# Picked layers of a four-layer residual kernel: loops over single steps, half-wide row hand-offs and single row and product buffers

## The chip, the cores and the metric

The kernel runs on one core of a Trainium2 chip. The metric is the device time of one execution in microseconds. Times of single instructions, waits and chains come from one profiled execution of the kernel.

## The reference, cut to what matters

`x` is 32 sequences of 64 rows of 1024 values. Four residual layers follow each other: `x + conv(x)` (a long convolution with a generated kernel), `x + x·W1[id1]ᵀ`, `x + x·W2[id2]ᵀ`, and a gated MLP with rank-16 adapters. The change touches the second and third, the "picked" layers:

```python
def _L1_cond_ref(x, adapter_ids, weight):
    w = weight[adapter_ids]                      # (32, 1024, 1024), one of 16 matrices per sequence
    return jnp.einsum('bsi,boi->bso', x, w)
...
x = x + _L1_cond_ref(x, itok_B_0_15, L1_cond_weight)
x = x + _L2_cond_ref(x, L2_cond_weight, itok_B_1_14)
```

Each sequence picks one of 16 matrices of 1024 x 1024. With the inputs that `setup_inputs(0)` draws, the picks are

```text
itok_B_0_15 12 10 13 8 7 5 2 8 12 3 7 3 15 8 2 1 12 12 7 10 13 9 8 14 7 11 10 14 8 0 8 10
            sequences per matrix 0..15: 1 1 2 2 0 1 0 4 6 1 4 1 4 2 2 1
itok_B_1_14 9 7 13 9 6 11 2 4 7 6 5 4 8 3 3 9 14 11 12 11 10 9 10 4 14 11 13 4 5 6 9 3
            sequences per matrix 0..15: 0 0 1 3 4 2 3 2 1 5 2 4 1 2 2 0
```

## The kernel before, in words

**Steps.** During the convolution VectorE builds a table on the chip: sequences with the same pick are put together in pairs, and each pair (or a left-over single one, with a spare sequence beside it) is a step. A step loads one matrix (4 MB, in four chunks of 1 MB) and multiplies the 2 x 64 = 128 rows of its pair with it. A table line per layer holds the matrix and the two places in `X` for every step; lines beyond the last real step point at spare rows and at matrix 0. `count_turns` (L1244 on) finds the number of **turns**, of two steps each, as the highest step number halved and rounded up. All engines loop over turns, with `half` 0 and 1 in a turn.

**Arithmetic.** Each fp32 factor is cut into a high part (ScalarE: `wh`, `rh`, one copy to the type for fast matmuls) and the rest (VectorE: `wl`, `rl`, a subtraction); TensorE adds up three products, high·high, high·low and low·high. A chunk is 4 blocks of 128 x 512, so 12 matmuls of 512 columns; a step is 48.

**A step on each engine, before.**
- SP (L387 to L402) waits for VectorE's cut of the same chunk of the step before (`w_lo`) and loads the chunk into `W[:, c]`.
- ScalarE (`picked_turn`, L758): cut chunk 0 (L741), cut the rows of the step (L755, two activations of 128 x 512), copy the first half of the last step's product out of PSUM (L746), cut chunk 1, copy the second half, cut chunks 2 and 3.
- VectorE: cut chunk 0 (L1302), the rows (L1315, two), chunks 1 and 2, add the last step's result to `X` (L1325, two), chunk 3.
- TensorE (`picked_turn`, L1766): chunk 0, eight transposes of the last step's product (L1762), chunks 1, 2, 3.

The host lays the matrix out so that chunks 0 and 1 make the first half of the output and chunks 2 and 3 the second; each output half has a PSUM bank, and `rh`, `rl`, `prod` and these banks exist twice, for `half` 0 and 1. The rows are therefore needed whole from chunk 0 on, and the rows' second half is read up to chunk 3. The order of the work is the order written in each engine's program; the engines meet through counting semaphores. `step_added` holds ScalarE back from the rows of the next layer until the last step of this one is in `X`.

**After the picked layers** `rows_done` (L1332) releases two 4 MB stores of `X` on SP, and ScalarE and VectorE begin to cut the MLP's operands. POOL sets the identity matrix for the transposes when the convolution ends.

Of the kernel before, what the change touches and what calls it, by code (L numbers as in the profile page):

```python
# [48 lines left out]
assert STEPS % 2 == 0 and STEPS <= B  # L49
# [74 lines left out]
def build(nc, ins, out):  # L124
    with ExitStack() as ctx:
# [24 lines left out]
        turns = sb(early, "turns", [2, 1], I32)  # L150
# [43 lines left out]
        with ExitStack() as s:  # L194
            ident = sb(s, "ident", [P, P])
            wh = sb(s, "wh", [P, WC, WK, WN], F32R)
            wl = sb(s, "wl", [P, WC, WK, WN], F32R)
            rh = sb(s, "rh", [P, 2, LT, 2 * H], F32R)
            rl = sb(s, "rl", [P, 2, LT, 2 * H], F32R)
            prod = sb(s, "prod", [2 * H, 2, L])  # L200
            sb(s, "gap", [P, (region + REGION - nc.sbuf_base) // 4])
            W = sb(s, "W", [P, WC, WK, WN])
# [86 lines left out]
        turned = sem("turned")  # L289
        step_added = sem("step_added")  # L290
# [55 lines left out]
        def _(sp):  # L346
# [44 lines left out]
            for layer, w in enumerate((ins["w1"], ins["w2"])):  # L391
                count = sp.value_load(turns[layer:layer + 1, 0:1], min_val=B // 4, max_val=STEPS // 2)
                with sp.Fori(0, count) as it:
                    for half in range(2):
                        pick = sp.value_load(table[layer:layer + 1, 0, bass.ds(it * 2 + half, 1)],
                                             min_val=0, max_val=NPICK - 1)
                        for c in range(WC):

                            sp.wait_ge(w_lo, (it * 2 + (before + half)) * WC + (c + 1))
                            sp.dma_start(W[:, c], w[bass.ds(pick, 1), c].rearrange("a p i o -> (a p) i o")  # L400
                                         ).then_inc(w_in[c], 16)
                before = before + count * 2  # L402
# [303 lines left out]
        def _(act):  # L706
# [36 lines left out]
            def copy_product(g, half, o):  # L743

                act.wait_ge(chunk_done, g * WC + (2 * o + 2 + WC))
                nc.scalar.activation(prod[:, half, o * WN:(o + 1) * WN], bank(2 * half + o),  # L746
                                     ACT.Copy).then_inc(prod_copied, 1)

            def step_rows_hi(s, half, added):

                seqs = [act.value_load(table[layer:layer + 1, 1 + k, bass.ds(s, 1)],
                                       min_val=0, max_val=B + SPARE - 1) for k in range(2)]
                act.wait_ge(step_added, added)
                for k, seq in enumerate(seqs):
                    nc.scalar.activation(rh[:, half, :, k * H:(k + 1) * H],  # L755
                                         X[:, bass.ds(seq, 1)].rearrange("p a l h -> p (a l) h"),
                                         ACT.Copy).then_inc(rows_hi, 1)

            def picked_turn(it, base, first):

                for half in range(2):
                    s = it * 2 + half
                    g = base + s
                    lag = not (first and half == 0)
                    if lag:
                        cut_chunk(g, 0)
                        step_rows_hi(s, half, g + 1)
                        copy_product(g - 1, 1 - half, 0)
                    cut_chunk(g, 1)
                    if lag:  # L770
                        copy_product(g - 1, 1 - half, 1)
                    cut_chunk(g, 2)
                    cut_chunk(g, 3)
# [3 lines left out]
            for layer in range(2):  # L777
                count = act.value_load(turns[layer:layer + 1, 0:1], min_val=B // 4, max_val=STEPS // 2)
                step_rows_hi(0, 0, base + 2)
                if layer == 0:  # L780
                    cut_chunk(0, 0)
                picked_turn(0, base, True)
                with act.Fori(1, count) as it:
                    picked_turn(it, base, False)
                base = base + count * 2
                copy_product(base - 1, 1, 0)
                if layer == 0:
                    cut_chunk(base, 0)
                copy_product(base - 1, 1, 1)
# [268 lines left out]
        def _(dve):  # L1058
# [185 lines left out]
            def count_turns():  # L1244
# [41 lines left out]
            stages = [number_steps, count_turns, find_members, place_members]  # L1286
# [8 lines left out]
            V.memset(tick[:, 2:3], 0.0).then_inc(chunk_done, WC)  # L1295
            V.memset(tick[:, 3:4], 0.0).then_inc(step_added, 2)
# [8 lines left out]
            def place(s, k):  # L1305
                return dve.value_load(table[layer:layer + 1, 1 + k, bass.ds(s, 1)],
                                      min_val=0, max_val=B + SPARE - 1)

            def step_rows_lo(s, g, half):

                for k in range(2):
                    seq = place(s, k)
                    dve.wait_ge(rows_hi, g * 2 + (k + 1))
                    mine = slice(k * H, (k + 1) * H)
                    V.tensor_tensor(out=rl[:, half, :, mine],  # L1315
                                    in0=X[:, bass.ds(seq, 1)].rearrange("p a l h -> p (a l) h"),
                                    in1=rh[:, half, :, mine].bitcast(F32), op=ALU.subtract).then_inc(rows_cut, 1)

            def add_step(s, g):

                for k in range(2):
                    seq = place(s, k)
                    dve.wait_ge(turned, g + 1)
                    rows = X[:, bass.ds(seq, 1)].rearrange("p a l h -> p (a l) h")
                    ins_ = V.tensor_tensor(out=rows, in0=ps[:, TURN:TURN + 2].rearrange(  # L1325
                        "p c (l w) -> p (c l) w", w=2 * H)[:, :, k * H:(k + 1) * H], in1=rows, op=ALU.add)
                ins_.then_inc(step_added, 1)

            dve.wait_ge(table_ready, 1)
            base = 0  # L1330
            for layer in range(2):
                count = dve.value_load(turns[layer:layer + 1, 0:1], min_val=B // 4, max_val=STEPS // 2)  # L1332
                step_rows_lo(0, base, 0)
                if layer == 0:
                    cut_chunk(0, 0)
                for half in range(2):
                    if half == 1:
                        cut_chunk(base + 1, 0)
                        step_rows_lo(1, base + 1, 1)
                    cut_chunk(base + half, 1)  # L1340
                    cut_chunk(base + half, 2)
                    if half == 1:
                        add_step(0, base)
                    cut_chunk(base + half, 3)
# [705 lines left out]
```

## Time and profile before

| | us |
|---|---|
| median of 3 runs (2216.17 to 2218.48) | 2217.92 |
| the profiled execution, its own time | 2217.24 |
| its span | 2215.6 |
| TensorE busy, share of the span | 96% |
| VectorE busy, share of the span | 73% |

TensorE's clock is given as a share of full speed. TensorE's mean granted clock over the run was 0.99. "Idle before, releaser" in a row is the time that the engine had nothing to run before the instruction, and what ended it; the chain of waits follows the work back from the last instruction, each piece with the time by which it moved the end. Matmuls overlap each other, so in the timeline each seems to last longer than the distance to the next one; the chain shows the distance.

### The profile page before, as it was taken

The page shows a single profiled execution, that of the slowest core. Times are in us where ns is not written, and L with a number is a line of the kernel's source. Part 1 is how long each engine was busy: PE and PEld are TensorE (multiplying, and loading weights), DVE is VectorE, ACT ScalarE, POOL GpSimd, SP SyncE. Part 2 cuts the span into 40 slices and gives each one's busy share as a digit, 9 for nine tenths or more (in the row PEclk, how much of TensorE's full clock was granted, in tenths as well). Part 3 has the DMA queues.
Part 4 walks back from the last instruction along what each step waited for, and adds up shares of the span by engine and source line. Part 5 has one row for each costly group of instructions (what it writes and reads, how often), then busy time and mean ns, then how long its engine had stood idle before and what let it go on. Part 6 is the DMA issues. An engine that isn't in the chain of part 4 may idle for free.

```text
span 2215.6 us, 33884 instructions
## 1 busy us (share of the span) xinstructions
PE 2118.8 (96%) x10544; PEld 1793.9 (81%) x10544; DVE 1625.9 (73%) x2079; ACT 975.7 (44%) x1222; POOL 98.9 (4%) x167
## 2 busy tenths in 40 slices
PE   2998999999998799999999999999999999999998
PEld 2997888878886688888888778888888888878887
DVE  7778999989997887878787336548888878753433
ACT  2222877777784533434333324334343433333332
POOL 3111000000000231000000000000000000000000
PEclk9999999999998999999999999999999999999999
DMA  5999999989997575434343895534434343365543
GB/s 192 380 363 351 349 352 352 355 306 351 352 354 302 159 203 146 108 94 113 93 111 101 250 261 189 185 121 110 107 95 107 95 106 101 84 199 171 181 152 123
DMA packets 255813, 449.90 MB, mean 203 GB/s; under 512 B 147031, under 2 KB 147223, under 8 KB 234519
## 3 DMA queue, kind: packets, MB, share of 16 engines
q1 hardware_dynamic: 242198, 417.08, 57.4%
q0 software_dynamic: 11392, 32.01, 4.4%
q10 hardware_dynamic: 2176, 0.26, 0.1%
q8 instruction: 21, 0.34, 0.1%
q14 instruction: 26, 0.20, 0.0%
HBM read 409.13 MB, written 63.73 MB: 213 GB/s over the span
## 4 chain that ended last, share of the span: by engine, by line
PE 83%; DVE 7%; SPq 3%; DMA 2%; issue 2%; ACT 2%; DVEq 0%; POOL 0%; ACTq 0%; POOLq 0%
PE ps L1791 18%; PE ps L1792 18%; PE ps L1793 18%; PE ps L1752 7%; PE ps L1754 7%; PE ps L1753 7%; PE ps L1729 3%; SPq L529 2%; PE ps L1836 2%; PE ps L1835 2%; PE ps L1762 2%; PE ps L1867 1%; PE ps L1868 1%; DMA araw<-picked_a 1%; DMA wraw<-picked_bd 1%
## 5 line engine op out<-in xcount | busy, mean ns | idle before, releaser
L1791 PE MATMUL ps<-bh,oph 128*128 128x512 f32 x1216 | 476.4, 392 | 9.5 <-ACT tmp L793 6.0
L1792 PE MATMUL ps<-bl,oph 128*128 128x512 f32 x1216 | 475.9, 391 | 0.0
L1793 PE MATMUL ps<-bh,opl 128*128 128x512 f32 x1216 | 474.3, 390 | 0.0
L1302 DVE TENSOR_TENSOR wl<-W,wh 128x2048 fp32r<-128x2048 f32 x160 | 362.3, 2286 | 28.7 <-ACT wh L741 28.7
L1366 DVE TENSOR_TENSOR tmp<-ps,tmp 128x512 f32<-128x512 f32 (+1 forms) x340 | 234.3, 690 | 132.2 <-PE ps L1836 67.2
L1363 DVE TENSOR_TENSOR wdl<-wraw,wdh 128x1024 fp32r<-128x1024 f32 x92 | 112.7, 1225 | 268.6 <-ACT wdh L793 268.6
L741 ACT ACTIVATE wh<-W 128x2048 fp32r<-128x2048 f32 x160 | 299.0, 1908 | 7.2 <-DMA W<-in_w 5.6
L1791 PE MATMUL ps<-acb_h,wdh 128*128 128x512 f32 (+1 forms) x736 | 281.3, 382 | 7.5 <-DVE acb_l L1363 7.0
L1792 PE MATMUL ps<-acb_l,wdh 128*128 128x512 f32 (+1 forms) x736 | 279.8, 380 | 0.0
L1793 PE MATMUL ps<-acb_h,wdl 128*128 128x512 f32 (+1 forms) x736 | 279.6, 380 | 0.0
L1791 PEld LDWEIGHTS ps<-bh,oph 128*128 128x128 f32 x1216 | 229.5, 189 | 55.0 <-DVE opl L1363 10.7
L1793 PEld LDWEIGHTS ps<-bh,opl 128*128 128x128 f32 x1216 | 229.0, 188 | 48.7
L1752 PE MATMUL ps<-wh,rh 128*128 128x512 f32 x640 | 257.1, 402 | 11.8 <-DVE wl L1302 7.6
L1792 PEld LDWEIGHTS ps<-bl,oph 128*128 128x128 f32 x1216 | 229.6, 189 | 42.9
L1754 PE MATMUL ps<-wh,rl 128*128 128x512 f32 x640 | 251.1, 392 | 0.0
L1753 PE MATMUL ps<-wl,rh 128*128 128x512 f32 x640 | 250.7, 392 | 0.0
L793 ACT ACTIVATE wdh<-wraw 128x1024 fp32r<-128x1024 f32 x92 | 97.4, 1059 | 313.9 <-PE ps L1793 250.1
L793 ACT ACTIVATE oph<-sraw 128x512 fp32r<-128x512 f32 x168 | 106.1, 632 | 279.8 <-PE ps L1793 152.6
L1791 PEld LDWEIGHTS ps<-acb_h,wdh 128*128 128x128 f32 x736 | 138.4, 188 | 38.7 <-DVE acb_l L1363 6.5
L1793 PEld LDWEIGHTS ps<-acb_h,wdl 128*128 128x128 f32 x736 | 138.4, 188 | 26.6
L1792 PEld LDWEIGHTS ps<-acb_l,wdh 128*128 128x128 f32 x736 | 138.4, 188 | 25.7
L1752 PEld LDWEIGHTS ps<-wh,rh 128*128 128x128 f32 x640 | 121.1, 189 | 43.3 <-issue 19.9
(204 smaller groups left out, 2843.7 us busy)
## 6 DMA issues: line engine op xcount, KB each, us to landing
W<-in_w SPq DMA_DIRECT2D x160, 1024.0 KB, 4.9
raw<-in_wgu SPq DMA_DIRECT2D x168, 256.0 KB, 2.8
wraw<-in_wd SPq DMA_DIRECT2D x84, 512.0 KB
toep<-kpad SPq DMA_DIRECT2D x32, 1024.0 KB, 8.9
lraw<-picked_b SPq DMA_DIRECT2D x88, 256.0 KB, 4.1
raw<-kept_acts SPq DMA_DIRECT2D x88, 256.0 KB, 3.5
kept_acts<-tmp SPq DMA_DIRECT2D x84, 256.0 KB, 2.3
picked_b<-in_lora_b POOLq DMA_DIRECT2D x32, 352.0 KB, 4.7
```

The costliest lines, as they stand in the source:

```text
L741: nc.scalar.activation(wh[:, c], W[:, c], ACT.Copy).then_inc(w_hi, 1)
L793: return nc.scalar.activation(to, src, ACT.Copy)
L1302: V.tensor_tensor(out=wl[:, c], in0=W[:, c], in1=wh[:, c].bitcast(F32), op=ALU.subtract).then_inc(w_lo, 1)
L1363: return V.tensor_tensor(out=to, in0=a, in1=b, op=ALU.subtract)
L1366: return V.tensor_tensor(out=to, in0=a, in1=b, op=ALU.add)
L1729: last = mm(ps[:, i % RING, (e + 1) * LT * B - n:(e + 1) * LT * B], lhsT=toep[:, i % RING, e, d * P:(d + 1) * P], rhs=rows[:, 0:n], start= ...
L1752: mm(to, lhsT=rh[:, half, at], rhs=wh[:, c, k], start=first, stop=False)
L1753: mm(to, lhsT=rh[:, half, at], rhs=wl[:, c, k], start=False, stop=False)
L1754: last = mm(to, lhsT=rl[:, half, at], rhs=wh[:, c, k], start=False, stop=end)
L1791: mm(to, lhsT=wh, rhs=mh, start=start, stop=False)
L1792: mm(to, lhsT=wh, rhs=ml, start=False, stop=False)
L1793: return mm(to, lhsT=wl, rhs=mh, start=False, stop=stop)
```

## The change

- The loops of all engines run over single steps; `count_turns` becomes `count_steps`, the highest step number plus one. The assertion that the number of table lines is even goes.
- `rh`, `rl` and `prod` exist once; the product's two PSUM banks exist once. The identity matrix moves behind them in memory.
- The host lays the chunks out anew: chunks 0 and 1 hold the first half of the input dimension (for the two output halves), chunks 2 and 3 the second. So chunks 0 and 1 read the first half of the rows alone, 2 and 3 the second half, and output half `o` is complete after chunk `2 + o`.
- ScalarE and VectorE cut a step's rows in two halves (128 x 256 each, for two sequences: four instructions instead of two), each half once the chunks that read its old content are done.
- TensorE waits for the copy of product half `o` before it writes bank `o` again, and for both copies before the transposes.
- The last step of a layer is written out: four transposes stand inside chunk 3, ahead of its last block, VectorE adds this half to `X`, and ScalarE and VectorE cut the next layer's first row half while the second half of the product is still on its way. In the last step of the first layer they also cut the next layer's chunks 0 and 1 ahead.

```diff
+            rh = sb(s, "rh", [P, LT, 2 * H], F32R)      # rl alike
+            prod = sb(s, "prod", [2 * H, L])
 SP
-                with sp.Fori(0, count) as it:
-                    for half in range(2):
-                        pick = sp.value_load(table[layer:layer + 1, 0, bass.ds(it * 2 + half, 1)],
+                with sp.Fori(0, count) as it:
+                    pick = sp.value_load(table[layer:layer + 1, 0, bass.ds(it, 1)],
 ScalarE
+            def copy_product(g, o):
+                act.wait_ge(chunk_done, g * WC + (o + 3 + WC))
+                act.wait_ge(turned, g + 1)
+                nc.scalar.activation(prod[:, o * WN:(o + 1) * WN], bank(o), ACT.Copy).then_inc(prod_copied, 1)
+            def step_rows_hi(seqs, g, half):
+                act.wait_ge(chunk_done, g * WC + (2 * half + 2))
+                mine = slice(half * WK, (half + 1) * WK)
+                for k, seq in enumerate(seqs):
+                    nc.scalar.activation(rh[:, mine, k * H:(k + 1) * H],
+                                         X[:, bass.ds(seq, 1), mine].rearrange("p a l h -> p (a l) h"),
+                                         ACT.Copy).then_inc(rows_hi, 1)
+            def picked_step(it, g):
+                cut_chunk(g, 0)
+                seqs = places(it)
+                act.wait_ge(step_added, g + 1)
+                step_rows_hi(seqs, g, 0)
+                cut_chunk(g, 1)
+                copy_product(g - 1, 0)
+                cut_chunk(g, 2)
+                copy_product(g - 1, 1)
+                step_rows_hi(seqs, g, 1)
+                cut_chunk(g, 3)
...
+                else:                                   # the second layer's first step
+                    cut_chunk(base, 0)
+                    cut_chunk(base, 1)
+                    copy_product(base - 1, 0)
+                    act.wait_ge(half_added, 1)
+                    step_rows_hi(seqs, base, 0)
+                    copy_product(base - 1, 1)
+                    cut_chunk(base, 2)
+                    act.wait_ge(step_added, base + 2)
+                step_rows_hi(seqs, base, 1)
...
+                with act.Fori(1, count) as it:
+                    picked_step(it, base + it)
+            copy_product(base - 1, 0)                   # after both layers
+            copy_product(base - 1, 1)
 VectorE
-                link(V.tensor_scalar(found[:, 0, 0:1], found[:, 0, 0:1], 0.5, 0.75, ALU.mult, ALU.add))
-                round_turns(found[:, 0, 0:1])
-                link(V.tensor_copy(turns[:], found[:, 0, 0:1]))
+                link(V.tensor_scalar_add(found[:, 0, 0:1], found[:, 0, 0:1], 1.0))
+                link(V.tensor_copy(counts[:], found[:, 0, 0:1]))
...
+            V.memset(tick[:, 7:8], 0.0).then_inc(turned, 1)
+            V.memset(tick[:, 5:6], 0.0).then_inc(rows_cut, 2)
+            V.memset(tick[:, 4:5], 0.0).then_inc(prod_copied, 3)
...
+            def picked_step(it, g):
+                cut_chunk(g, 0)
+                both = places(it, layer)
+                step_rows_lo(both, g, 0)
+                cut_chunk(g, 1)
+                cut_chunk(g, 2)
+                step_rows_lo(both, g, 1)
+                add_step(it - 1, g - 1)
+                cut_chunk(g, 3)
...
+                last = places(count - 1, layer)
+                base = base + count
                 if layer == 0:
                     cut_chunk(base, 0)
+                    cut_chunk(base, 1)
+                add_last_half(last, 0, base - 1)
+                if layer == 0:
+                    both = places(0, 1)
+                    step_rows_lo(both, base, 0)
+                    add_last_half(last, 1, base - 1)
+                    cut_chunk(base, 2)
+                    step_rows_lo(both, base, 1)
+                    cut_chunk(base, 3)
+                else:
+                    add_last_half(last, 1, base - 1)
 TensorE
+            def picked_step(g, first=False, last=False):
+                pe.wait_ge(rows_cut, g * 4 + 4)
                 pe.wait_ge(prod_copied, g * 2 + 2)
+                chunk(g, 0)
+                if not first:
+                    turn_product(g - 1)                 # waits: prod_copied (both copies), step_added
+                pe.wait_ge(prod_copied, g * 2 + 3)
+                chunk(g, 1)
+                pe.wait_ge(rows_cut, g * 4 + 6)
+                chunk(g, 2)
+                if not last:
+                    chunk(g, 3)
+                    return
+                chunk(g, 3, range(WK - 1))
+                pe.wait_ge(prod_copied, g * 2 + 4)
                 pe.wait_ge(step_added, g + 2)
+                turn_half(0).then_inc(half_turned, 1)
+                chunk(g, 3, range(WK - 1, WK))
+                pe.wait_ge(prod_copied, g * 2 + 5)
+                turn_half(1).then_inc(turned, 1)
...
+                picked_step(base, first=True)
+                with pe.Fori(1, count - 1) as it:
+                    picked_step(base + it)
+                base = base + count
+                picked_step(base - 1, last=True)
 host
-    picked = lambda w: w.reshape(NPICK, 2, WN, 2, WK, P).transpose(0, 1, 3, 5, 4, 2).reshape(
+    picked = lambda w: w.reshape(NPICK, 2, WN, 2, WK, P).transpose(0, 3, 1, 5, 4, 2).reshape(
```

## Rows read from the trace of the kernel before

**Rows 1.** The page: busy time of each engine, share of the span, instructions.

```profile
PE 2118.8 (96%) x10544; PEld 1793.9 (81%) x10544; DVE 1625.9 (73%) x2079; ACT 975.7 (44%) x1222; POOL 98.9 (4%) x167
```

**Rows 2.** Groups by line (busy us, mean ns | idle before): picked layers.

```profile
L1302 DVE TENSOR_TENSOR wl<-W,wh 128x2048 fp32r<-128x2048 f32 x160 | 362.3, 2286 | 28.7 <-ACT wh L741 28.7
L741 ACT ACTIVATE wh<-W 128x2048 fp32r<-128x2048 f32 x160 | 299.0, 1908 | 7.2 <-DMA W<-in_w 5.6 <-PE ps L1754 1.0
...
L1315 DVE TENSOR_TENSOR rl<-X,rh 128x512 fp32r<-128x512 f32 x80 | 51.7, 685 | 2.8 <-ACT rh L755 2.5
L1325 DVE TENSOR_TENSOR X<-ps,X 128x512 f32 x80 | 51.5, 683 | 8.8 <-PE ps L1762 8.5 <-issue 0.3
L746 ACT ACTIVATE prod<-ps 128x512 f32<-128x512 f32 x80 | 47.2, 590 | 100.6 <-PE ps L1754 100.6
...
L1762 PE MATMUL ps<-ident,prod 128*128 128x128 f32 x320 | 41.5, 273 | 1.5 <-ACT prod L746 1.5
```

**Rows 3.** The page, DMA issues: count, size, median us to landing.

```profile
W<-in_w SPq DMA_DIRECT2D x160, 1024.0 KB, 4.9
```

**Rows 4.** Windows: us, busy us of each engine (instructions), PE clock, DMA share, GB/s.

```profile
210.00:225.00 15.00, 15.00 (x67) 12.37 (x67) 11.93 (x8) 10.39 (x9) 0.00 (x0) 0.93 0.98 375
...
300.00:443.00 143.00, 143.00 (x675) 117.33 (x674) 135.88 (x97) 111.52 (x95) 0.00 (x0) 1.00 0.95 353
443.00:455.00 12.00, 6.97 (x32) 5.37 (x31) 6.57 (x7) 5.92 (x6) 0.00 (x0) 0.84 0.60 228
```

**Rows 5.** Chain of waits, whole run (start us, us): the transposes of single steps.

```profile
224.16 0.88 PE ps L1762 x8
236.15 0.87 PE ps L1762 x8
247.93 0.87 PE ps L1762 x8
...
438.33 0.88 PE ps L1762 x8
```

**Rows 6.** Chain of waits, 303.5 to 309.5 us: around a step's first matmul.

```profile
304.37 0.23 PE ps L1754
304.59 0.34 PE ps L1752
```

**Rows 7.** Waits from 260 to 440 us: total us, times, longest us.

```profile
ACT prod L746 <- PE ps L1754: 34.3, 15, 2.5
DVE wl L1302 <- ACT wh L741: 9.4, 16, 0.7
```

**Rows 8.** Timeline of ScalarE, 440 to 475 us: the layers' border.

```profile
451.09 1.15 ACT L755 ACTIVATE rh<-X 128x512 fp32r x2 [3.05 <-DVE X L1325]
```

**Rows 9.** Timeline of VectorE, 440 to 475 us.

```profile
450.27 0.69 DVE L1325 TENSOR_TENSOR X<-ps,X 128x512 f32 x1 [0.16 <-issue]
```

**Rows 10.** Timeline of TensorE, 440 to 460 us.

```profile
447.02 0.39 PE L1754 MATMUL ps<-wh,rl 128*128 128x512 f32 x1
448.18 1.09 PE L1762 MATMUL ps<-ident,prod 128*128 128x128 f32 x8 [0.77 <-ACT prod L746]
453.53 0.79 PE L1752 MATMUL ps<-wh,rh 128*128 128x512 f32 x1 [4.26 <-DVE rl L1315]
```

**Rows 11.** Chain of waits, 440 to 475 us: TensorE after the border.

```profile
454.32 0.43 PE ps L1753
...
457.73 0.38 PE ps L1752
```

**Rows 12.** Timelines of ScalarE, then VectorE, 680 to 706 us: the end.

```profile
692.72 0.60 ACT L746 ACTIVATE prod<-ps 128x512 f32<-128x512 f32 x1 [4.84 <-PE ps L1754]
...
695.54 0.69 DVE L1325 TENSOR_TENSOR X<-ps,X 128x512 f32 x1 [0.17 <-issue]
```

**Rows 13.** Timeline of TensorE, 743 to 765 us: a gap in the next layer.

```profile
759.96 0.47 PE L1791 MATMUL ps<-bh,oph 128*128 128x512 f32 x1 [3.48 <-ACT tmp L793]
760.26 0.40 PE L1792 MATMUL ps<-bl,oph 128*128 128x512 f32 x1
```

More of the change, by code:

```diff
@@ L48 @@
 SPARE = 3
-assert STEPS % 2 == 0 and STEPS <= B
+assert STEPS <= B
 FF = 2752
@@ L1319, in add_step, with step_rows_lo @@
-            def add_step(s, g):
[L1321 to L1326, printed above, removed]
-                ins_.then_inc(step_added, 1)
+            def step_rows_lo(both, g, half):
+                lts = slice(half * WK, (half + 1) * WK)
+                for k, seq in enumerate(both):
+                    dve.wait_ge(rows_hi, g * 4 + (2 * half + k + 1))
+                    mine = slice(k * H, (k + 1) * H)
+                    V.tensor_tensor(out=rl[:, lts, mine],
+                                    in0=X[:, bass.ds(seq, 1), lts].rearrange("p a l h -> p (a l) h"),
+                                    in1=rh[:, lts, mine].bitcast(F32), op=ALU.subtract).then_inc(rows_cut, 1)
@@ new lines, in turned_rows @@
+            def turned_rows(seq, k, at, n):
+                rows = X[:, bass.ds(seq, 1), at * WK:(at + n) * WK].rearrange("p a l h -> p (a l) h")
+                return V.tensor_tensor(out=rows, in0=ps[:, TURN + at:TURN + at + n].rearrange(
+                    "p c (l w) -> p (c l) w", w=2 * H)[:, :, k * H:(k + 1) * H], in1=rows, op=ALU.add)
+            def add_step(s, g):
+                for k, seq in enumerate(places(s, layer)):
+                    dve.wait_ge(turned, g + 2)
+                    ins_ = turned_rows(seq, k, 0, 2)
+                ins_.then_inc(step_added, 1)
@@ new lines, in add_last_half, with places @@
+            def add_last_half(both, at, g):
+                if at == 0:
+                    dve.wait_ge(half_turned, layer + 1)
+                else:
+                    dve.wait_ge(turned, g + 2)
+                for k, seq in enumerate(both):
+                    ins_ = turned_rows(seq, k, at, 1)
+                ins_.then_inc(half_added if at == 0 else step_added, 1)
+            def places(s, at):
+                return [dve.value_load(table[at:at + 1, 1 + k, bass.ds(s, 1)],
+                                       min_val=0, max_val=B + SPARE - 1) for k in range(2)]
@@ L1742, in _ @@
                     convolve(c, i)
-            def chunk(g, half, c):
-                pe.wait_ge(w_lo, g * WC + (c + 1 + WC))
-                to = bank(2 * half + c // 2)
-                for k in range(WK):
-                    at = (c % 2) * WK + k
-                    first, end = at == 0, at == LT - 1
-                    mm(to, lhsT=rh[:, half, at], rhs=wh[:, c, k], start=first, stop=False)
-                    mm(to, lhsT=rh[:, half, at], rhs=wl[:, c, k], start=False, stop=False)
-                    last = mm(to, lhsT=rl[:, half, at], rhs=wh[:, c, k], start=False, stop=end)
-                last.then_inc(chunk_done, 1)
@@ L1780, in _ @@
             for layer in range(2):
[L1781 to L1786 removed]
+                count = pe.value_load(counts[layer:layer + 1, 0:1], min_val=B // 2, max_val=STEPS)
+                picked_step(base, first=True)
+                with pe.Fori(1, count - 1) as it:
+                    picked_step(base + it)
+                base = base + count
+                picked_step(base - 1, last=True)
             def three(to, wh, wl, mh, ml, start, stop):
```

156 lines of the change are left out of this document (56 added, 100 removed).

## The prediction

> **What bounds the kernel now.** I began with the page: TensorE is busy for 96% of the span, VectorE for 73% [rows 1]. A mean hides stages, so I took the groups by line next. A step of a picked layer asks VectorE for four chunk cuts of 2286 ns, two row cuts of 685 and two adds of 683: 11.88 us if nothing overlaps; and ScalarE for 4 x 1908 and 2 x 590 ns and two row copies [rows 2]. The 160 loads of W are 40 steps, landing 4.9 us after issue [rows 3], though the picks drawn need only 19 pairs in each layer (each matrix's count halved and rounded up: 19 and 19). So one step in each layer is padding. By the windows TensorE is busy without a break from 300 to 443 us, VectorE for 135.88 of 143 us, and DMA moves 353 GB/s; a window near by reached 375 GB/s, so the loads too have only some 6% in hand [rows 4]. The chain of waits shows which limit holds: from the transposes at 224.16 to those at 438.33 us lie 18 steps, 11.90 us each [rows 5], and the pieces between are matmuls of 0.23 us, with 0.34 at the start of a loop turn [rows 6]. Steady steps are bound by TensorE. VectorE still has about 0.6 us of waiting in each (9.4 us in 15 steps), ScalarE 2.3 [rows 7]. At the border of the layers TensorE stands: ScalarE waits for VectorE's last add before it may cut rows [rows 8], which ends at 450.96 us [rows 9]; TensorE's last matmul starts at 447.02 and the next layer's first at 453.53, 6.51 us later, with eight transposes inside [rows 10]. The granted clock of that window is 0.84 [rows 4], and ten matmuls run at about 0.43 instead of 0.23 us, from 453.53 to 458.11 [rows 10, 11]: the lower level, 1.2 GHz.
>
> **The change, part by part.**
>
> *Steps.* Two of 40 steps go, TensorE's and their loads with them: 2 x 11.90 = **-23.8 us**. The padding did full work: all steps have the same length [rows 5].
>
> *Loop turns.* Every step now begins a turn, every second one did. An interval with a turn's start was 11.99 us, one without 11.78 [rows 5]; over the 18 the mean lies about 0.07 below the long ones, and the first matmul of a turn costs 0.34 - 0.23 = 0.11 us [rows 6]. TensorE also gets one more wait before chunk 0, one before chunk 1 and one before chunk 2, all on things long done; the trace has no such wait alone, so its price lies between 0 and the 0.11 of a turn's start. I take 0.1 a step for all, near the turn row: 36 x 0.1 = **+3.5 us** (0 to +8).
>
> *VectorE in a step.* Rows in halves are two instructions more. On the line through 685 ns for 512 columns and 2286 for 2048 a half takes 419 ns, fixed part 152 [rows 2]. The row sums to 11.88, yet a step of 11.90 holds 0.6 of waiting [rows 2, 5, 7], so neighbours overlap by about 0.6 over eight instructions, 0.08 each; the two extra cost 2 x (0.15 - 0.08) = 0.15 us, and busy time becomes 11.4 of 11.9. Cost nothing while 0.5 us is left. Counting from a step's start on TensorE, with matmul chunks of 2.7 and transposes of 0.9 us [rows 5, 6]: transposes end at 3.7, VectorE adds until 5.1, cuts chunk 3 until 7.3, the next step's chunk 0 until 9.5, row half 0 until 10.2, chunk 1 until 12.4, chunk 2 until 14.6 and row half 1 until 15.3, which is 3.4 in the next step, before its transposes. TensorE wants chunk 0 at 11.9, row half 1 and chunk 2 at 18.3, chunk 3 at 21.0. The cover is TensorE's own work, 2 us or more everywhere.
>
> *ScalarE in a step.* A half row copy is about 0.37 us on the line through 590 and 1908 ns [rows 2]; four are 1.5 us, and the 2.3 us of waiting hold what is added. The copy of product half 0 moves behind chunk 2 (9.3 to 9.9 us after the step's start), ahead of the bank's new use at 11.9; then chunk 2's cut until 11.8, just 0.6 before VectorE takes it. Product half 1 is complete at 12.1 and copied at 12.7; the transposes want it at 14.6. Behind it stand the second row half and chunk 3's cut, done by 15.3; VectorE takes it at 17.0. So the single buffers and banks cost 0. If ScalarE were 0.6 us later, VectorE would begin to wait.
>
> *Loads.* As many bytes a step, one queue, the same wait for VectorE's cut. By the times above chunk loads are issued at 9.5, 12.4, 14.6 and 19.2 us (before, the add stood between the last two in the same way). At 375 GB/s a chunk takes 2.8 us [rows 4], four 11.2 of 11.9; with 4.9 to landing chunk 0 lands just before ScalarE asks for it and VectorE 2 us behind that. Cost 0, at most 0.2 a step. SP's one register load a step stays.
>
> *The border.* Now half the product is turned inside chunk 3, and ScalarE and VectorE have cut the next chunks 0 and 1. From the end of the first four transposes: two half adds with their start 1.05 us, two half row copies 0.95, copy of product half 1 0.55 (it stands behind them on ScalarE), hand-over 0.15, four slow transposes 0.55 (half of 1.09 [rows 10]) and TensorE's load of the new count, some 0.25. That is 3.5 us; the four transposes and the last block put its beginning at about the old last matmul's start. Against 6.51: **-3.0 us** (-1.5 to -4). VectorE's row half is done before product half 1 is turned; late next is that copy.
>
> *The clock at the border.* TensorE's pause falls from 0.77 and 4.26 us around the transposes [rows 10] to one of about 2. The low stretch cost 4.58 us for ten matmuls, at 0.23 each 2.3 [rows 11]: **-2.2 us** if it goes, 0 if not. I take that it goes, by the nearest row below.
>
> *The end.* Before, 3.51 us from the start of the last copies (692.72) to the last add's end (696.23) [rows 12]. After: 0.44 for transposes put into chunk 3, 0.60 copy, 0.12, 0.55 transposes, 0.14, two half adds of 0.42 with the 0.17 between them [rows 12], 2.85 in all: **-0.7 us** (0 to -1.3). The MLP hangs on this add; its loads wait behind the stores of `X` released by it, so it moves as a whole.
>
> *The beginning.* Three memsets more and one register load more ahead of the first row cut, half as much row work before the first matmul: 0 (-0.5 to +0.5). The table gets shorter by some small operations, hidden by the convolution's last tiles. The moved identity is written by POOL at the same place in its queue; nothing waits for it before the second step.
>
> **Sum:** -23.8 + 3.5 - 3.0 - 2.2 - 0.7 = -26.2 us. The profiled execution took 2217.24, so 2191.0; it lies 0.7 under the median of 2217.92, so I predict **2191.7 us** for the median.
>
> **On the clock.** After a pause of 3.48 us at 759.96 the matmuls of the next layer keep 0.40 us each, as those at 447.02 do [rows 10, 13]; after 0.77 plus 4.26 with small transposes between they fall to the low level. A pause of 2 us is on the safe side of both.
>
> **Rivals.**
> 1. *The clock still falls at the border.* For: the transposes around the pause are already slow. Against: rows 13. 2191.7 + 2.2 = 2193.9.
> 2. *VectorE becomes the bound.* If nothing of its work overlapped, a step would be 4 x 2.286 + 4 x 0.419 + 2 x 0.683 = 12.18 us, 0.28 more, 38 x 0.28 = 10.7: 2202. Against: overlap is what rows 2 and 7 show together.
> 3. *Slower: the single row and product buffers put hand-overs in line.* Place: ScalarE's row copies behind the last step's product. Price: at the border, where that order is forced, add end to first matmul is 453.53 - 450.96 = 2.57 us [rows 9, 10]; in each of 38 steps it is 98 us: 2289. It decides from 26.2 / 38 = 0.7 us a step. Against: the cover of 2 us worked out above. The Trainium skill (Trainium Kernel Development and Optimization, Best Practices) asks for double buffers to overlap DMA with compute, which speaks against the change; W keeps its four chunks a step ahead, and no row shows a second row buffer in use for more than this cover.
> 4. *A turn's start gets dear.* If smaller loops fetched code at each turn, and a fetch took what the loads here take, 4.9 us [rows 3], 36 of them would be 176 us: about 2368. Against: 0.11 us at 18 such starts [rows 6]. The Trainium skill (Runtime: NRT & Kernel Launch, Instruction fetch mechanics) says that a taken branch to code outside the sequencer's window stalls for a fetch; the trace shows no such stall before.
> 5. *No step is saved* (other picks than drawn by seed 0, or a count of 20). Then 40 steps and the rest: -3.0 - 2.2 - 0.7 + 3.7 = -2.2: 2215.7, within 0.2%, which is about what a measurement of this kernel can tell from no change.
>
> **Chances.** Forecast 0.74, rival 1 0.08, rival 2 0.10, rival 3 0.02, rival 4 0.02, rival 5 0.04. Faster by over 0.2% 0.92, within 0.04, slower 0.04. Range: the low end takes turn starts at 0 and the border at its best (2187), the high end the dearer waits or rival 2 (2203).
>
> **What would show it.** 152 loads of W and 1824 matmuls of 512 columns in the picked layers; steps of 11.9 to 12.0 us between transposes; VectorE's waits now before the adds (for the transposes), some 0.5 us a step; about 3.5 us between the first layer's last matmul and the second's first, at full clock; the rest of the kernel shifted by 26 us. Steps of 12.2 with VectorE never waiting would be rival 2; TensorE waiting for row cuts or the product copy in each step, rival 3. 160 loads would overthrow the main term.

## The result, and the profile after

The changed kernel takes 2185.36 us (median of 4 runs, 2185.11 to 2187.31) against 2217.05 us for the kernel before in the same comparison (4 runs, 2214.07 to 2218.48): a ratio of 0.9853, 95% interval 0.9842 to 0.9865, so 31.7 us less, where 26.2 were forecast. The profiled execution took 2185.16 us.

The page of the changed kernel (span, busy time of the engines, the loads of W), which answers to [rows 1, 3]:

```profile
span 2183.5 us, 34214 instructions
...
PE 2087.3 (96%) x10432; PEld 1774.5 (81%) x10432; DVE 1610.3 (74%) x2144; ACT 971.2 (44%) x1282; POOL 99.0 (5%) x167
...
W<-in_w SPq DMA_DIRECT2D x152, 1024.0 KB, 6.9
```

152 loads are 38 steps: the main term is there. But a load now lands 6.9 us after its issue, not 4.9. The groups by line, answering to [rows 2], say who notices:

```profile
L1318 DVE TENSOR_TENSOR wl<-W,wh 128x2048 fp32r<-128x2048 f32 x152 | 343.6, 2285 | 9.9 <-ACT wh L742 9.0
...
L742 ACT ACTIVATE wh<-W 128x2048 fp32r<-128x2048 f32 x152 | 290.7, 1915 | 61.0 <-DMA W<-in_w 55.1 <-PE ps L1795 3.6
...
L1327 DVE TENSOR_TENSOR rl<-X,rh 128x256 fp32r<-128x256 f32 x152 | 57.3, 418 | 3.1 <-issue 2.3 <-ACT rh L759 0.7
...
L748 ACT ACTIVATE prod<-ps 128x512 f32<-128x512 f32 x76 | 44.4, 584 | 10.7 <-PE ps L1795 9.3
```

Read the right-hand side. ScalarE's wait for TensorE before the product copies fell from 100.6 us to 9.3, VectorE's for ScalarE's chunk cuts from 28.7 to 9.0, and ScalarE's wait for loads rose from 5.6 to 55.1. The half row cuts take 418 ns, as worked out. The chain of waits gives the pace, answering to [rows 5]:

```profile
225.62 0.87 PE ps L1802 x8
237.41 0.87 PE ps L1802 x8
249.19 0.87 PE ps L1802 x8
...
303.26 7.93 DMA W<-in_w
```

A step is 11.79 us (from one set of transposes to the next, and the same as mean of the 17 up to 425.89 us), not 11.9 to 12.0 as forecast, and not 11.90 as before. From 303 us on the chain runs through loads of W: they have become as late as they may be.

The border of the layers, in the timelines of TensorE, ScalarE and VectorE of the changed kernel (answering to [rows 8 to 10]):

```profile
434.35 0.65 PE L1802 MATMUL ps<-ident,prod 128*128 128x128 f32 x4
434.76 0.47 PE L1793 MATMUL ps<-wh,rh 128*128 128x512 f32 x1
438.12 0.66 PE L1802 MATMUL ps<-ident,prod 128*128 128x128 f32 x4 [2.43 <-ACT prod L748]
439.17 0.49 PE L1793 MATMUL ps<-wh,rh 128*128 128x512 f32 x1 [0.39 <-issue]
...
440.00 0.63 PE L1793 MATMUL ps<-wh,rh 128*128 128x512 f32 x1
```
```profile
431.82 1.92 ACT L742 ACTIVATE wh<-W 128x2048 fp32r<-128x2048 f32 x1 [0.72 <-DMA W<-in_w]
433.65 0.58 ACT L748 ACTIVATE prod<-ps 128x512 f32<-128x512 f32 x1
436.86 0.72 ACT L759 ACTIVATE rh<-X 128x256 fp32r x2 [2.64 <-DVE X L1334]
437.49 0.58 ACT L748 ACTIVATE prod<-ps 128x512 f32<-128x512 f32 x1
```
```profile
433.77 2.29 DVE L1318 TENSOR_TENSOR wl<-W,wh 128x2048 fp32r<-128x2048 f32 x1 [0.34 <-ACT wh L742]
435.98 0.75 DVE L1334 TENSOR_TENSOR X<-ps,X 128x256 f32 x2
```

From the last matmul of layer one (435.30) to the first of layer two it is 3.87 us against 6.51; forecast, 3.5. The half add could have begun at 435.0, when the four transposes were done. It began at 435.98, behind the cut of the next layer's chunk 1, which was late because its load was. The pause is short, and still TensorE falls to its lower clock level (matmuls 0.43 us apart instead of 0.23) 0.8 us after it has started again.

### The profile page after: what moved, and what is told of

Read it like the earlier page. It is cut to its first block, busy times and chain, and to the rows that moved or that the text cites. A ratio compares the mean times of both kernels' runs of the same rounds, so it can differ in the third digit from the quotient of the medians.

```text
span 2183.5 us, 34214 instructions
## 1 busy us (share of the span) xinstructions
PE 2087.3 (96%) x10432; PEld 1774.5 (81%) x10432; DVE 1610.3 (74%) x2144; ACT 971.2 (44%) x1282; POOL 99.0 (5%) x167
## 4 chain that ended last, share of the span: by engine, by line
PE 82%; DVE 8%; DMA 4%; ACT 2%; issue 2%; DVEq 1%; POOL 0%; ACTq 0%; SPq 0%; POOLq 0%
PE ps L1849 19%; PE ps L1850 19%; PE ps L1851 19%; PE ps L1793 4%; PE ps L1795 4%; PE ps L1794 4%; PE ps L1769 4%; DMA W<-in_w 3%; PE ps L1894 2%; PE ps L1893 2%; DVE wl L1318 2%; PE ps L1802 1%; PE ps L1925 1%; PE ps L1926 1%; DMA araw<-picked_a 1%
## 5 line engine op out<-in xcount | busy, mean ns | idle before, releaser
L1318 DVE TENSOR_TENSOR wl<-W,wh 128x2048 fp32r<-128x2048 f32 x152 | 343.6, 2285 | 9.9 <-ACT wh L742 9.0
L742 ACT ACTIVATE wh<-W 128x2048 fp32r<-128x2048 f32 x152 | 290.7, 1915 | 61.0 <-DMA W<-in_w 55.1
L1793 PE MATMUL ps<-wh,rh 128*128 128x512 f32 x608 | 242.4, 399 | 7.9 <-DVE wl L1318 7.5
L1795 PE MATMUL ps<-wh,rl 128*128 128x512 f32 x608 | 238.8, 393 | 0.0
L1794 PE MATMUL ps<-wl,rh 128*128 128x512 f32 x608 | 238.3, 392 | 0.0
L807 ACT ACTIVATE oph<-sraw 128x512 fp32r<-128x512 f32 x168 | 106.1, 632 | 282.5 <-PE ps L1851 154.2
L1769 PE MATMUL ps<-urev,toep 128*128 128x256 f32 (+7 forms) x1024 | 150.5, 309 | 1.7 <-issue 1.2
```

The costliest lines, as they stand in the source:

```text
L742: nc.scalar.activation(wh[:, c], W[:, c], ACT.Copy).then_inc(w_hi, 1)
L807: return nc.scalar.activation(to, src, ACT.Copy)
L1318: V.tensor_tensor(out=wl[:, c], in0=W[:, c], in1=wh[:, c].bitcast(F32), op=ALU.subtract).then_inc(w_lo, 1)
L1769: last = mm(ps[:, i % RING, (e + 1) * LT * B - n:(e + 1) * LT * B], lhsT=toep[:, i % RING, e, d * P:(d + 1) * P], rhs=rows[:, 0:n], start= ...
L1793: mm(bank(o), lhsT=rh[:, at], rhs=wh[:, c, k], start=first, stop=False)
L1794: mm(bank(o), lhsT=rh[:, at], rhs=wl[:, c, k], start=False, stop=False)
```

## The experiments

"Picked layers" below is the time from their first matmul to the release of the MLP (the memset of `tick` in VectorE's timeline), "border" the distance between the layers' matmuls, "slow" the matmuls more than 0.35 us apart among the first 60 after it, "MLP" from the release to the span's end. All come from the one profiled execution of each run, the medians from all its executions. e1 to e8 ran on one chip, e9 to e11 on another; for the first pair (before, changed) the chip is not on record.

| kernel | us a step | picked layers | border | slow | MLP | median, and that of before beside it |
|---|---|---|---|---|---|---|
| before | 11.90 | 487.6 | 6.51 | 10 | 1519.3 | 2217.05 |
| e1 before again | 11.90 | 487.3 | 6.50 | 9 | 1517.1 | 2219.54, 2220.31 |
| e2 chunk 2's cut ahead | 11.80 | 484.9 | 6.51 | 8 | 1517.4 | 2216.35, 2220.31 |
| changed | 11.79 | 457.9 | 3.87 | 8 | 1516.4 | 2185.36, 2217.05 |
| e3 20 steps | 11.80 | 481.3 | 3.38 | 8 | 1521.2 | 2212.20, 2220.31 |
| e4 plain border | 11.79 | 460.8 | 5.75 | 14 | 1520.5 | 2191.42, 2220.31 |
| e5 changed again | 11.79 | 457.7 | 3.78 | 7 | 1516.8 | 2185.86, 2218.86 |
| e6 copy first | 12.04 | 466.6 | 3.80 | 9 | 1519.3 | 2198.90, 2218.86 |
| e7 border reordered | 11.82 | 456.8 | 2.83 | 8 | 1520.1 | 2188.31, 2218.86 |
| e8 three loads | 11.79 | 455.7 | 2.94 | 7 | 1520.7 | 2186.25, 2218.86 |
| e9 changed, third | 11.79 | 455.8 | 3.56 | 0 | 1522.0 | 2190.64, 2219.81 |
| e10 late release | 11.79 | 455.6 | 2.94 | 0 | 1518.2 | 2187.98, 2219.81 |
| e11 e7 again | 11.80 | 455.8 | 2.92 | 0 | 1519.8 | 2185.78, 2219.81 |

**The lead.** In the kernel before the steady step cost 0.1 us too much, and I had charged that to the loop's turn. These rows of its timelines (VectorE, TensorE's weight loads, ScalarE; the last column says what ended the idle time) show one step around 304 to 316 us:

```profile
304.63 0.60 ACT L746 ACTIVATE prod<-ps 128x512 f32<-128x512 f32 x1 [2.37 <-PE ps L1754]
...
305.12 5.51 ACT L741 ACTIVATE wh<-W 128x2048 fp32r<-128x2048 f32 x3
...
307.06 2.29 DVE L1302 TENSOR_TENSOR wl<-W,wh 128x2048 fp32r<-128x2048 f32 x1 [0.57 <-ACT wh L741]
...
309.27 1.28 DVE L1325 TENSOR_TENSOR X<-ps,X 128x512 f32 x2
...
310.47 4.48 DVE L1302 TENSOR_TENSOR wl<-W,wh 128x2048 fp32r<-128x2048 f32 x2
...
314.88 1.29 DVE L1315 TENSOR_TENSOR rl<-X,rh 128x512 fp32r<-128x512 f32 x2
...
316.29 0.19 PEld L1752 LDWEIGHTS ps<-wh,rh 128*128 128x128 f32 x1 [0.18 <-issue]
```

The row cuts end at 316.17 and the next step's first weights are loaded at 316.29, after 0.18 us of idle time. The profile names no releaser for it ("issue"). In the list of waits from 260 to 440 us it comes back in most steps:

```profile
PEld ps L1752 <- issue: 3.1, 13, 0.3
```

Two comparisons say that this is the wait for the row cuts. From 230 to 430 us the first weight load of a step starts 0.12 to 0.13 us after VectorE's last row cut in every step, in both profiles of the kernel before; in e2 below it starts 0.49 to 0.61 us after it in all steps but the last, and the idle time is gone. So there is a ring: last matmul of a step, copy of the second product half, chunk 2's cut behind it on ScalarE, VectorE's cut, adds, two more cuts, row cuts, first matmul. It leads from the last matmul of one step to the first of the step after the next, so it fixes the length of two steps together and not of each: any two neighbouring intervals in the chain of [rows 5] add up to 23.8 us (23.76 to 23.83), while single ones lie between 11.77 and 11.99. The same chain of waits shows that the long ones don't follow the loop. Early in the layer the 1st, 3rd and 5th intervals are long; here, at its end, the 16th and the 18th (11.97), with a 17th of 11.82:

```profile
402.57 0.87 PE ps L1762 x8
414.54 0.87 PE ps L1762 x8
426.36 0.87 PE ps L1762 x8
438.33 0.88 PE ps L1762 x8
```

Turns begin at every second step from the first to the last, so a turn's price can't move from odd to even intervals.

**e2: only one line of the kernel before moved.**

```diff
                     cut_chunk(g, 1)
+                    cut_chunk(g, 2)
                     if lag:
                         copy_product(g - 1, 1 - half, 1)
-                    cut_chunk(g, 2)
```

> The kernel before with one line moved on ScalarE: the cut of chunk 2 stands ahead of the copy of the second product half. Theory 'cycle': before, a step hung on a ring: last matmul, copy of the second product half, cut of chunk 2, VectorE's four cuts and two adds, row cuts, next step's first matmul; the move takes the copy out of it, steps fall from 11.90 to 11.79 us, 38 x 0.11 = 4 us less in all. Theory 'loop turn' (what I predicted with): the 0.11 us is the price of a turn of the loop on TensorE; nothing changes, 11.90 us a step and 0 us in all.

The steps fall to 11.80 us; the chain of waits of e2:

```profile
286.22 0.87 PE ps L1762 x8
298.00 0.87 PE ps L1762 x8
309.80 0.87 PE ps L1762 x8
```

and the ratio to before is 0.9979 (0.9970 to 0.9987), 4.0 us between the medians (3.2 against e1). The picked layers of its profile are only 2.4 to 2.7 us shorter than in the two profiles before; its first 60 matmuls took 1.1 to 1.3 us longer there, 13 of them slow, and its last steady step of layer one 12.08 us. (VectorE's cuts in the ring are three, not the four of the expectation.) Loops still turn every second step here and every step in the changed kernel, and both take 11.79 to 11.80 us: a turn costs 0.01 us or less. Its waits from 260 to 440 us (total us, times, longest), beside [rows 7]:

```profile
ACT wh L741 <- DMA W<-in_w: 26.0, 32, 1.8
ACT prod L746 <- PE ps L1754: 5.5, 10, 0.8
...
DVE wl L1302 <- ACT wh L741: 1.1, 3, 0.7
```

The 9.4 us in which VectorE waited for ScalarE have gone to 1.1, and the waits for loads appear here too: they belong to the faster pace, not to the single buffers.

**e6: the old order put back into the changed kernel.**

```diff
                 copy_product(g - 1, 0)
+                copy_product(g - 1, 1)
                 cut_chunk(g, 2)
-                copy_product(g - 1, 1)
                 step_rows_hi(seqs, g, 1)
```

> The changed kernel with the old order on ScalarE in the loop: the copy of the second product half ahead of chunk 2's cut. Theory 'order': this order alone closes the ring through ScalarE and VectorE again, steps go back to about 11.9 to 12.0 us and the kernel is 34 x 0.1 to 0.2 = 3.5 to 7 us slower. Theory 'buffers': the half-wide rows and the new chunk order opened the ring, and steps stay at 11.79.

Steps of 12.04 us, in pairs (297.60, 309.73, 321.65 in its chain: 12.13 and 11.92), picked layers 8.9 us longer than e5's (36 steps of the loop x 0.25 = 9.0). "Order" it is, somewhat dearer than thought. In its waits from 225 to 430 us the ring shows again, at both of its joints:

```profile
ACT prod L748 <- PE ps L1795: 27.7, 16, 2.1
DVE wl L1318 <- ACT wh L742: 12.8, 18, 2.9
...
PEld ps L1793 <- issue: 5.9, 17, 0.5
```

So with chunk 2's cut ahead, half-wide rows and single buffers neither cost nor gain anything in steady steps (11.79 with them, 11.80 without, in e2); the place of one copy in ScalarE's program does. With the copy ahead they aren't free: 12.04 us against the 11.90 of the kernel before. The medians are 13.0 us apart, the profiles' picked layers 8.9; the other 4 us are no more than executions of one program differ by (below), but no run assigns them.

**e3: padding.** `count_steps` adds 2.0 instead of 1.0.

> The changed kernel with one padding step added to each layer, so 40 steps as before. If the steps taken away carry the gain at 11.8 us each, this is 23.6 us slower than the changed kernel (2208.9 against 2185.4) and the rest, some 8 us, stays ahead of the kernel before. If padding were cheaper than a real step it would be less.

The steps are 11.80 us long, so two are 23.6 us, as expected. Picked layers are 481.3 us against 457.9 and 457.7 in the first two profiles of the changed kernel, 23.4 and 23.6 more (25.5 more than in e9, which has no slow matmul at the border). The medians lie 26 us apart across two comparisons.

**e4: the last step of a layer like the others.** TensorE's part of the edit (ScalarE copies both halves and then waits for the whole step's add; VectorE uses `add_step`):

```diff
-                picked_step(base - 1, last=True)
+                picked_step(base - 1)
+                turn_product(base - 1)
```

> The changed kernel with the last step of each layer as the others are: whole product turned after chunk 3, both halves added at once, rows of the next layer cut after that. Theory 'border': 2.5 us more between the first layer's last matmul and the second's first (6.5 against 4.0), and 0.7 us more at the end, so about 3.2 us slower than the changed kernel, with the low clock as long as before. If the clock's low stretch hangs on the pause, up to 0.5 us more.

Picked layers 460.8, so 2.9 to 3.1 us more than in the first two profiles of the changed kernel (5.0 more than in e9); border 5.75, with 14 slow matmuls instead of 7 or 8. The size is right. The split was not: 1.9 from the border's distance where 2.5 were expected, about 0.6 at the end (last matmul to release 3.73 us against 2.70, less 0.44 for the transposes inside chunk 3), the rest clock. The medians, 2191.42 against 2185.36 and 2185.86, are 5.6 to 6.1 us apart, with a range of 9.3 us in e4's four executions: they give the sign and not the size.

**e8: a quarter of the loads left out.** Chunk 3 is loaded once and its old content used in all steps, so the product is not that of the picked matrices.

```diff
+            sp.wait_ge(w_lo, WC)
+            sp.dma_start(W[:, WC - 1], ins["w1"][0, WC - 1]).then_inc(w_in[WC - 1], 16)
...
-                    for c in range(WC):
+                    for c in range(WC - 1):
```

> The changed kernel with chunk 3 loaded once, not in every step: a quarter of the matrix bytes is left out of every step, so the product is that of an old chunk 3. Theory 'TensorE bounds the step': steps stay at 11.79 us although ScalarE's waits for loads (28 us over 17 steps) go. Theory 'loads bound it', since W is now in the chain of waits: steps fall below 11.7. In either case the half add at the border comes up to 1 us earlier, because chunk 1 is no longer late: border gap 2.9 to 3.3 instead of 3.9.

Windows from 296 to 430 us of e5 (first) and e8 (second), each in its own fence, with DMA share and GB/s at the end:

```profile
296.00:430.00 134.00, 134.00 (x641) 111.93 (x639) 130.67 (x116) 111.21 (x112) 0.00 (x0) 1.00 0.94 353
```
```profile
296.00:430.00 134.00, 134.00 (x636) 111.79 (x635) 130.09 (x114) 109.83 (x112) 0.00 (x0) 1.00 0.72 268
```

DMA share falls from 0.94 to 0.72, ScalarE's waits for loads go (2.3 us in all, none from 225 to 430 us), and the step stays at 11.79: TensorE bounds it, the loads are in the chain only because they end together with it. At the border the half add is no longer behind a late chunk (2.94 us, as expected). e10, which loads everything and leaves the border as it is, has the same 2.94 us, because its chunk 1 was cut in time: VectorE ends that cut at 433.85 and adds the half from 433.89 on, just after the four transposes are done (433.75):

```profile
429.36 4.49 DVE L1318 TENSOR_TENSOR wl<-W,wh 128x2048 fp32r<-128x2048 f32 x2
433.89 0.76 DVE L1334 TENSOR_TENSOR X<-ps,X 128x256 f32 x2
```

So the border of the unchanged order is 2.94 us with timely loads and up to 3.87 with a late one.

**e7 and e11: the border in another order.**

```diff
 ScalarE
                     copy_product(base - 1, 0)
+                    copy_product(base - 1, 1)
                     act.wait_ge(half_added, 1)
                     step_rows_hi(seqs, base, 0)
-                    copy_product(base - 1, 1)
 VectorE
                     cut_chunk(base, 0)
-                    cut_chunk(base, 1)
                 add_last_half(last, 0, base - 1)
...
                     add_last_half(last, 1, base - 1)
+                    cut_chunk(base, 1)
                     cut_chunk(base, 2)
```

> The changed kernel with another order at the border: ScalarE copies the second product half before it waits for the half add; VectorE adds the half and cuts the next layer's first row half before it cuts the next chunk 1. Theory 'a late chunk cut holds the half add, and the copy stands behind it': the distance from the first layer's last matmul to the second's first falls from 3.9 to about 2.3 us, 1.5 us faster in all, if VectorE's later cuts are not missed at chunks 1 and 2 (up to 0.4 us lost again). If TensorE's clock falls for the pause, less than 8 slow matmuls; if it falls anyway, 8 to 14 as in the profiles so far.

> The kernel of e7 again. Picked layers 456.8 us or, without the late loads of that execution, 455.8; border gap 2.8. If its MLP is again 1520 against 1516.6 of the changed kernel on the same chip, the 3 us belong to the program, not to the execution, and they hide the 1 to 2 us that the border gains.

The border takes 2.83 and 2.92 us, 0.6 to 1.0 less than in the changed kernel's three profiles (3.87, 3.78, 3.56), not the 1.5 hoped for, and hardly less than the 2.94 of e10 with the old order. What the new order does is to take the half add out from behind the late chunk: it gains up to 1 us when a load is late there and 0.1 or less when none is. Picked layers take 456.8 and 455.8 us, against 457.9, 457.7 and 455.8. In both, single steps lost time in the loop that this edit doesn't touch (longest 12.41 and 12.02; in e7 the chain of waits runs through loads of W there). The medians, 2188.31 beside 2185.86 and 2185.78 beside 2190.64, say nothing either way. e11's MLP, 1519.8 us, repeats e7's 1520.1, which its expectation would have put down to the program; but e9, the changed kernel on the same chip, has 1522.0, so it decides nothing.

**e1, e5, e9, e10: what an execution of the same program varies by.**

> The kernel before, unchanged, for a second profile. The first layers must agree with the first profile: 11.90 us a step, 6.5 us at the border. The question is the MLP: from ScalarE's first cut of the MLP's rows to the span's end the kernel before took 1519.2 us, the changed one 1516.3. Theory 'the MLP varies by execution': this profile differs from 1519.2 by one us or more with the same program. Theory 'the change moved it': 1519.2 again within 0.5.

> The changed kernel, unchanged, for its median beside the variants on one chip and for a second profile. The picked layers must agree with the first: 11.79 us a step, 457.9 us from the first matmul to the release of the MLP within 1.5. Theory 'the MLP varies by execution': its 1516.4 us of the first profile come out another way, between 1516 and 1522 as in the five other profiles. Theory 'the change moved the MLP': 1516.4 again within 0.5.

> The changed kernel a third time, beside the next two on one chip. Picked layers 457.7 to 457.9 us again. MLP: 'one value for one program' says 1516.4 to 1516.8 as in the two profiles so far; 'by execution' says anything from 1516 to 1521.

e10 puts this before the release:

```diff
+            for k in range(LT):
+                V.memset(rl[:, k].bitcast(F32), 0.0)
             V.memset(tick[:, 6:7], 0.0).then_inc(rows_done, 1)
```

> The changed kernel with eight small memsets (128 x 128) between the last add and the release of the MLP, some 1 to 1.5 us. Theory 'the MLP follows its release as a whole': the MLP takes 1516.4 to 1516.8 us and all of it ends that much later. Theory 'its load-bound stretches fall differently with any shift or other program': units unchanged at 457.5 us, but the stretch before them or the first panels change by 1 to 5 us, as between the other profiles.

The changed kernel gives an MLP of 1516.4, 1516.8 and 1522.0 us, the kernel before 1519.3 and 1517.1: the program doesn't fix it, and e5 alone would have misled me. The 1522.0 is also the only one of the three from the other chip, so for the profiles alone "by chip" would do as well as "by execution". The times of all executions settle that much: on one chip e5's four span 2183.59 to 2193.45 us and e1's ten 2213.28 to 2221.88, 9 to 10 us for one program. Which part of the kernel they differ in, only a profile shows. Here are the releases in the timelines of VectorE, of the changed kernel and of e9:

```profile
667.09 0.06 DVE L1399 MEMSET tick<- 1x1 f32 x1
```
```profile
664.78 0.06 DVE L1399 MEMSET tick<- 1x1 f32 x1
```

Released 2.3 us earlier, e9 ends 3.3 later (spans of 2183.5 and 2186.8 us). The adapters' matmuls (L1925 and L1926) mark the MLP's two loops over units: from the first to the last of a loop it is 458.3 to 458.5 us in all profiles (once 458.9, in e2). What moves is the stretch from the release to the first of them (66.8 to 70.4) and the one from the first loop to the second (282.5 to 288.6), where weights for the down projection are loaded beside the next rows. ScalarE's waits for those loads over the whole execution, in the changed kernel and in e9 (the changed kernel has none for `picked_bd`):

```profile
ACT wdh L807 <- DMA wraw<-in_wd: 50.6, 13, 4.3
```
```profile
ACT wdh L807 <- DMA wraw<-in_wd: 53.9, 14, 4.8
ACT wdh L807 <- DMA wraw<-picked_bd: 9.3, 2, 4.8
```

e10's MLP took 1518.2 us, within that scatter, so whether a shift of the release alone moves it can't be told from e10. Nor did it come down to a fixed MLP with a later end, which the first theory wanted (1516.4 to 1516.8).

## Why the prediction was right or wrong

**Steps: right.** -23.8 forecast; 23.6 by e3, and 152 loads instead of 160, so rival 5 didn't come.

**Loop turns, +3.5: wrong in sign, and this is the step that failed.** I read the 0.34 us at the first matmul of a step, and the long and short intervals, as the price of a turn, put +0.1 us on each of 36 steps, and called steady steps "bound by TensorE". They were, but for 0.1 us a step that came from the ring through the second product copy. Turns cost 0.01 us or less (rival 4 didn't come either), and the change opened the ring by moving that copy behind chunk 2's cut: 38 steps, 11.90 - 11.79 each, give -4.1. The error of this term is 7.6 us, more than the 5.5 by which the whole forecast fell short. The low end of the range had turns at 0 but nothing for the ring, and so 2187 lay above the 2185.36 measured. Two readings went with it: the prediction put the mean 0.07 us under the long intervals (11.99 - 11.90 is 0.09), and it took the first two intervals of [rows 5] for the pattern of all 18, where long and short change places. Its mark was on record in [rows 7]: ScalarE idle for 2.3 us a step ahead of a copy, and VectorE idle behind ScalarE. I had counted that idle time as room for the change to use. It was time lost to an order, and the sum of VectorE's rows, 11.88 us against a step of 11.90, should have made me follow what it waits for and who waits for it around the whole step.

**VectorE, ScalarE and the buffers at 0: right.** Half cuts at 418 ns, no wait of TensorE for rows in the steady steps of the changed kernel, and by e6 the schedule worked out in the prediction was the one that mattered, with chunk 2's cut ahead of copy two. Steps of 11.79 us leave no room for rival 2 (VectorE the bound, 12.18) nor for rival 3 (hand-overs in line).

**Loads at 0 in the step: right (e8), but they are nearer than I took them.** 6.9 us to landing, and at the border a late load holds the half add by about 1 us (3.87 us against e10's 2.94).

**The border, -3.0: size a little off.** 6.51 to 3.87 is -2.6, less 0.4 for the transposes that moved into chunk 3: -2.2. What is missing is the late load: with e10's 2.94 us the same sum gives -3.2. e4 has border, end and clock together at 3 us.

**The clock at the border, -2.2: not in the executions measured first.** 10 slow matmuls before, 8, 7 and then 0 in three profiles of the changed kernel; two fewer are worth -0.4. A pause of 2.43 us and less was not "on the safe side": e8 with a pause of 1.59 us before the second transposes still has 7, e9 with 2.21 us none. The prize is 1.6 to 2 us (the 60 matmuls after the border take 14.5 us in e9, 16.1 in the changed kernel, 16.6 before), and some profiles have it: rival 1, the clock still falls, held in the others. All three profiles with 0 slow matmuls (e9, e10, e11) are from one chip, and all eight on the other have 7 to 14, the kernel before included. Whether the chip or the execution decides stays open; no profile of the kernel before was taken on the chip with 0, so it isn't shown either that the shorter pause gains anything there.

**The end, -0.7:** from last matmul to release 3.99 us before (692.30 to 696.29), 2.69 after (664.40 to 667.09), less 0.44: -0.9.

**The beginning, 0:** the first 60 matmuls take 16.1 and 15.9 us in two profiles before and 17.0 to 17.2 in three after, because 12 or 13 instead of 7 or 8 are slow; e2, with the old buffers, has 13 as well, e7 9, e8 7. About +1, and not shown to belong to the change.

Together -23.6 - 4.1 - 2.2 - 0.9 - 0.4 + 1.0 = -30.2, against -29.7 for the picked layers in the two first profiles (487.6 to 457.9). That the whole was off by 5.5 and not by more is partly luck: border, clock and beginning came out 3.6 us dearer than forecast and hid nearly half of the 7.6. **The rest of 31.7:** the first pair of profiles also differs by 2.9 us in the MLP, in which three profiles of one program differ by themselves (up to 5.6). The three comparisons gave 31.7, 33.0 and 29.2 us less. Whether any of it beyond the picked layers belongs to the change stays open; nothing here requires it.

## What to carry to other kernels

When two engines' busy time and the bounding engine's step agree within a per cent, don't call the rest overlap: follow one step around the ring, from a wait to the wait behind it, and ask of each idle stretch ahead of a copy whether independent work could stand in it. Look also whether long and short steps keep their places in the loop before the loop gets the blame. Here moving one cut ahead of one copy was worth 4 us, without any of the new buffers. And before a difference of a few microseconds in an untouched stage is explained, profile the same program twice more, both programs on the same chip.

## What the runs showed of the hardware that I had not expected

The granted clock after a short pause is not a matter of the pause's length alone. e8 and e10 have the same pauses at the border, 1.59 us ahead of the second set of four transposes and 0.3 us behind it, and of the 60 matmuls that follow 7 are slow in e8 and none in e10. Windows of 8 us around the pause in e8 (first) and e10 (second) end in granted clock, DMA share and GB/s; the clock is 0.79 in the one and 1.00 in the other:

```profile
434.00:442.00 8.00, 6.52 (x23) 5.07 (x24) 6.65 (x8) 6.69 (x8) 0.00 (x0) 0.79 0.63 243
```
```profile
435.00:443.00 8.00, 6.67 (x30) 5.41 (x31) 6.79 (x9) 7.29 (x9) 0.00 (x0) 1.00 0.69 256
```

e7 and e11, one program, have 8 and 0. In both pairs the chip differs as well. The slow pace can begin after the pause has ended, as at 440.00 us in the changed kernel, where the first three matmuls still ran at the higher level. And a short hold of TensorE for another engine's work (0.1 to 0.35 us of idle time in the kernel before, up to 0.5 in e6) shows in the profile as "issue" of the weight load, with no releaser named.
